# A macaron transformer block: outer FFN tiles and layer tiles driven by one tick counter, new orders, squared chunks summed by TensorE

## The reference

```python
x = x + 0.5 * ffn(layernorm(x), w_up, w_down)
x = x + layers(layernorm(x), ...)
x = x + 0.5 * ffn(layernorm(x), w_up, w_down)

def ternary_linear(x, w):            # the outer FFN's linear
    alpha = mean(abs(w))
    w_q = sign(w) * (abs(w) > 0.5 * alpha)
    rms = sqrt(sum(x * x, -1)) / sqrt(d)
    return (x / (rms + 1e-8)) @ w_q.T
# ffn: h = gelu(ternary_linear(x, w_up)); ternary_linear(h, w_down); 128 -> 512 -> 128

# each of the 8 layers:
Q, K = elu(x @ Wq + bq) + 1, elu(x @ Wk + bk) + 1
value = x @ Wv + bv
KV, Ksum = sum(K * value, 1), sum(K, 1)
V = Q * KV / (Q * Ksum + 1e-6)
x = ln(gelu(V @ Wo + bo) + x)
x = ln(gelu(gelu(x @ W1 + b1) @ W2 + b2) + x)
```

## Time and profile before

| | us |
|---|---|
| median of 3 runs | 959.16 (956.42 to 959.33) |
| the profiled execution's own time | 957.2 |
| its span, first to last instruction | 955.4 |
| busy: PE, DVE, ACT, POOL | 868.9, 870.9, 832.9, 515.1 |
| first outer FFN, until the first layer product | 0 to 101.3 |
| layers, until the last z | 101.3 to 867.0 |
| second outer FFN | 867.0 to 955.4 |

### The profile page before, as it was taken

One profiled execution on the slowest core, in us unless ns is written; L12 is line 12 of the kernel. 1 busy time (PEld: TensorE's weight loads), 2 busy tenths in 40 slices (PEclk: granted clock), 3 DMA queues, 4 the chain that ended last, 5 costly groups with the idle time before them and its releaser, 6 DMA issues.

```text
span 955.4 us, 14548 instructions
## 1 busy us (share of the span) xinstructions
PE 868.9 (91%) x3915; PEld 595.7 (62%) x3915; DVE 870.9 (91%) x3421; ACT 832.9 (87%) x1214; POOL 515.1 (54%) x617
## 2 busy tenths in 40 slices
PE   3986579999999999999999999999999999995887
PEld 2876336666666666666666666666666666553787
DVE  6999669999999999999999999999999999967883
ACT  2754679999999999999999999999999999983653
POOL 4887413555555545555555555455445544554774
PEclk9999679999999999999999999999999999996998
DMA  5000000000000000000000000000000000000011
GB/s 156 1 2 1 25 9 1 1 15 21 1 1 15 21 1 1 15 21 0 1 14 21 1 15 1 20 0 15 1 12 1 1 1 1 0 1 1 12 34 46
DMA packets 19520, 12.07 MB, mean 13 GB/s; under 512 B 1160, under 2 KB 18288, under 8 KB 19440
## 3 DMA queue, kind: packets, MB, share of 16 engines
q1 hardware_dynamic: 19440, 11.13, 4.1%
HBM read 9.03 MB, written 2.10 MB: 12 GB/s over the span
## 4 chain that ended last, share of the span: by engine, by line
ACT 73%; DVE 8%; POOL 7%; PE 6%; issue 5%; DMA 0%; POOLq 0%; SPq 0%; DVEq 0%; ACTq 0%
ACT h L656 16%; ACT x_fm L671 9%; ACT L656 8%; ACT rec L633 6%; ACT rec L642 4%; ACT L679 4%; ACT L697 4%; ACT e_k L623 4%; ACT e_k L616 4%; ACT bank L649 4%; ACT bank L663 3%; ACT e_q L623 3%; ACT e_q L616 2%; DVE z L779 2%; PE bank L368 2%
## 5 line engine op out<-in xcount | busy, mean ns | idle before, releaser
L1167 POOL TENSOR_TENSOR x_lo<-x_fm,x_hi 128x512 fp32r<-128x512 f32 x128 | 172.4, 1347 | 257.3 <-DVE x_hi L932 257.3
L456 PE MATMUL bank<-h,w 128*128 128x512 f32 x512 | 261.1, 593 | 0.5 <-ACT h L656 0.5
L779 DVE TENSOR_SCALAR z<-bank,mv,rstd 128x128 f32<-128x128 f32 x512 | 171.9, 402 | 17.3 <-POOL rstd L1159 17.1
L656 ACT ACTIVATE h<-bank,par 128x512 f32<-128x512 f32 x256 | 170.6, 696 | 1.5 <-PE bank L376 0.6
L374 PE MATMUL bank<-x_hi,w_hi 128*128 128x512 f32 x256 | 159.7, 624 | 13.2 <-ACT h L656 10.2
L1159 POOL TENSOR_TENSOR rstd<-ve,minus_half 128x4 f32<-128x4 f32 x128 | 139.7, 1092 | 10.7
L456 PEld LDWEIGHTS bank<-h,w 128*128 128x128 f32 x512 | 91.7, 190 | 31.5 <-issue 16.5
L765 DVE BATCH_NORM_STATS2 st<-bank 128x6 f32<-128x128 f32 x512 | 111.2, 278 | 0.0
L374 PE MATMUL bank<-x_hi,wqkv_hi 128*128 128x512 f32 x192 | 97.0, 505 | 9.6 <-DVE phi_k L850 7.2
L671 ACT ACTIVATE x_fm<-bank,par 128x512 f32<-128x512 f32 x128 | 97.8, 789 | 7.3 <-PE bank L368 7.3
L376 PE MATMUL bank<-x_hi,w_lo 128*128 128x512 f32 x256 | 101.4, 396 | 0.0
(11 more groups left out here) (105 smaller groups left out, 1924.7 us busy)
## 6 DMA issues: line engine op xcount, KB each, us to landing
x_tm<-in_x SPq DMA_DIRECT2D x8, 256.0 KB, 3.9
raw_w<-in_W SPq DMA_DIRECT2D x8, 256.0 KB, 2.7
w<-in_W SPq DMA_DIRECT2D x8, 256.0 KB, 2.9
out<-x_tm SPq DMA_DIRECT2D x8, 256.0 KB, 2.3
raw_qkv<-in_Wk SPq DMA_DIRECT2D x8, 64.0 KB, 2.5
raw_qkv<-in_Wq SPq DMA_DIRECT2D x8, 64.0 KB, 2.3
raw_qkv<-in_Wv SPq DMA_DIRECT2D x8, 64.0 KB, 2.2
wo<-in_Wo SPq DMA_DIRECT2D x8, 64.0 KB, 2.5
```

The costliest lines, as they stand in the source:

```text
L456: mm = pe.matmul(m.ps_o[:, :], m.w2[T.weights][:, c, :], m.h[:, T.par, c, :], start=c == 0, stop=c == FC - 1)
L656: act.activation(m.h[:, T.par, c, :], m.ps_h[c % 2][:, :], ACT.Gelu_apprx_tanh, bias=column(m, B1, T.layer, c, FC)).then_inc(s.gelu_h[T.pa ...
L779: last = dve.tensor_scalar(dst[:, j, :], src(j), mv[:, j, 0:1], scale[:, j:j + 1], ALU.subtract, ALU.mult)
L1167: pool.tensor_tensor(m.x_lo[:, T.slot, :], m.x_fm[:, T.slot, :], m.x_hi[:, T.slot, :].bitcast(F32), ALU.subtract).then_inc(done, 1)
```

## The change

All three phases now run in one loop over ticks, from FIRST_TICK = -31 to END_TICK = 74, in one function per engine. `l(k, lag)` gives a layer tile, `a(k, lag)` a tile of the first outer FFN and `b(k, lag)` one of the second, two tiles to a tick in each; the lists are new in all of them. The squared chunks are no longer added by GpSimd: `squares` on TensorE accumulates over 16 products of 128x1. The normalisation ahead of the up-products is a scale and a shift on ScalarE (`normal`), with a new `shift` on VectorE. The gelus of the outer FFN have their own buffer fh; hsq is single; the down-products use ps_o alone, in two halves. Who must have emptied a bank is kept in `left` by the build. The exp table is loaded only if another was used. The rounding and x_lo behind the last layer are left out. In the layers the mean of V is one sum and one product.

```diff
+TICKS_IN = NT // 2
+TICK_W1 = 0
+FIRST_TICK, END_TICK = -31, 74
...
+def tiles_of(tick, f):
+    def l(k, lag):
         job = 2 * (tick - lag) + k
         return Tile(job) if 0 <= job < JOBS else None
+    def a(k, lag):
+        t = 2 * (tick - lag + TICKS_IN) + k
+        return Outer(f[0], t) if 0 <= t < NT else None
+    def b(k, lag):
+        t = 2 * (tick - lag - TICKS) + k
+        return Outer(f[1], t) if 0 <= t < NT else None
...
-            if T.n == 1:
-                pe.wait_ge(s.par_ready, 1)
-                pe.wait_ge(f[0].x_new, NT)
-                pe.wait_ge(f[0].ms, NT)
-        pe.wait_ge(s.x_split, T.n)
+        if T.layer == 0:
+            pe.wait_ge(f[0].x_split, T.n)
+        else:
+            pe.wait_ge(s.x_split, T.n - NT)
...
+    def outer_down(F, half):
+        if half == 0:
+            emptied(pe, left, "o")
+            left["o"] = (F.f.x_new, F.n)
+        pe.wait_ge(F.f.gelu[F.par], F.chunks + FC)
+        for j in (2 * half, 2 * half + 1):
+            for c in range(FC):
+                last = pe.matmul(m.ps_o[:, j * P:(j + 1) * P], m.fh[:, F.par, c, j * P:(j + 1) * P],
+                                 m.downT[:, c, :], start=c == 0, stop=c == FC - 1)
...
+    def squares(F):
+        emptied(pe, left, "q")
+        left["q"] = (F.f.ms, F.n)
+        pe.wait_ge(F.f.hsq, F.n)
         for j in range(BLK):
-            last = pe.matmul(m.ps_v[:, j:j + 1], m.hss[:, t % 2, j * P:(j + 1) * P], m.ones[:, 0:1],
-                             start=True, stop=True)
+            for c in range(FC):
+                last = pe.matmul(m.ps_q[:, j:j + 1], m.hsq[:, c, j * P:(j + 1) * P], m.ones[:, 0:1],
+                                 start=c == 0, stop=c == FC - 1)
...
+def load_exp_and_ln(act, tables):
+    if tables["now"] != EXP_AND_LN:
+        act.preload_act_table_set(EXP_AND_LN)
+    tables["now"] = EXP_AND_LN
...
+    def normal(F):
+        at_least(act, F.f.turned_z, F.n - 2)
+        act.wait_ge(F.f.shift, F.n)
+        sc = m.scale[:, F.par]
+        for j in range(BLK):
+            last = act.activation(m.fz[:, F.par, j, :], m.x_tm[:, F.t, j, :], ACT.Identity,
+                                  bias=sc[:, SHIFT, j:j + 1], scale=sc[:, ALPHA, j:j + 1])
+    def square(F):
+        at_least(act, F.f.ssq, F.n - 1)
+        act.wait_ge(F.f.gelu[F.par], F.chunks + FC)
+        act.activation(m.hsq[:, :, :], m.fh[:, F.par, :, :], ACT.Square).then_inc(F.f.hsq, 1)
...
-        for b in range(2):
-            last = dve.tensor_scalar(m.neg_a[:, T.par, b:b + 1], m.kvacc[:, T.par, b:b + 1], m.nrk[:, T.par, b:b + 1],
-                                     column(m, BV, T.layer), ALU.mult, ALU.subtract)
-        last.then_inc(s.neg_a, 1)
+        dve.tensor_tensor(m.neg_a[:, T.par, :], m.kv[:, T.par, :], m.nrk[:, T.par, :], ALU.mult).then_inc(s.neg_a, 1)
     def hi(T, i):
-        if not T:
+        if not T or i == 1 and T.layer == LAYERS - 1:
...
-        pool.tensor_tensor(total, sq[:, 0, :], sq[:, 1, :], ALU.add).then_inc(f.part_sums, 1)
-        pool.wait_ge(f.part_sums, 2 * t + 1)
-        pool.tensor_tensor(total, total, sq[:, 2, :], ALU.add).then_inc(f.part_sums, 1)
-        pool.wait_ge(f.part_sums, 2 * t + 2)
-        pool.tensor_tensor(total, total, sq[:, 3, :], ALU.add).then_inc(f.hss, 1)
```

More of the change, by code:

```diff
@@ L394, in tensor_engine, with emptied, tensor_tick, project @@
     pe.wait_ge(s.ternary_kept, 2)
[L396 to L405, removed]
+    left = {"k": (s.par_kept, 1)}
+    for tick in range(FIRST_TICK, END_TICK):
+        tensor_tick(pe, m, s, f, tick, left)
+def emptied(pe, left, bank):
+    if bank in left:
+        at_least(pe, *left[bank])
+def tensor_tick(pe, m, s, f, tick, left):
+    l, a, b = tiles_of(tick, f)
+    def project(T, i):
         if not T:
@@ new lines, in squares, with turn_c @@
+        last.then_inc(F.f.ssq, 1)
+    def turn_c(F):
+        if not F:
+            return
+        emptied(pe, left, "tz")
+        left["tz"] = (F.f.x_hi, F.n)
+        pe.wait_ge(F.f.z_c, F.n)
+        transpose_tile(pe, m.ps_tz, lambda j: m.fz_c[:, F.par, j, :], m).then_inc(F.f.turned_c, 1)
+    project(l(0, 0), KEY)
+    outer_up(a(0, -26), 1)
+    outer_down(a(0, -25), 1)
+    squares(b(1, 38))
+    up(l(1, 3), 3)
+    turn_c(a(1, -22))
+    turn_y(l(1, 2), 0)
+    down(l(1, 3), 0)
+    turn_y(l(0, 3), 1)
@@ L596, in scalar_engine @@
+    outer_up(a(1, -26), 1)
+    down(l(0, 2), 1)
+    turn_c(a(0, -23))
+    up(l(1, 2), 0)
+    turn(a(0, -27))
+    down(l(0, 2), 2)
+    outer_up(a(1, -26), 2)
+    project_o(l(1, 1))
+    outer_up(a(1, -26), 3)
+    outer_down(b(0, 37), 1)
+    squares(a(0, -26))
+    outer_up(a(0, -27), 0)
+    up(l(1, 2), 1)
+    down(l(0, 2), 3)
+    up(l(1, 2), 2)
+    turn_z(l(1, 3), 1)
+    turn_z(l(0, 1), 0)
+    outer_down(a(0, -26), 0)
 def scalar_engine(act, m, s, f):
@@ new lines, in scalar_tick @@
+    negative(l(0, 0), QUERY)
+    recip(l(1, 1))
+    gelu(b(0, 38), 3)
+    normal(b(0, 37))
+    exp(l(0, 0), QUERY)
+    gelu_h(l(0, 2), 0)
+    gelu_ff(l(1, 3))
+    square(a(0, -25))
+    gelu_h(l(0, 2), 1)
+    gelu(a(1, -25), 0)
+    full(l(1, 2), 0)
+    full(l(0, 3), 1)
+    gelu_o(l(0, 1))
+    gelu_h(l(0, 2), 2)
+    gelu(a(1, -25), 1)
+    square(b(0, 38))
+    gelu(b(1, 38), 0)
+    gelu(a(1, -25), 2)
+    negative(l(1, 0), KEY)
+    gelu_h(l(0, 2), 3)
+    exp(l(1, 0), KEY)
+    negative(l(1, 0), QUERY)
@@ new lines, in scalar_tick @@
+    log_den(l(0, 0))
+    gelu(b(1, 38), 1)
+    exp(l(1, 0), QUERY)
+    z_hi(a(0, -26))
+    gelu(a(1, -25), 3)
+    z_hi(b(0, 37))
+    gelu(b(1, 38), 2)
+    gelu(b(1, 38), 3)
+    gelu_h(l(1, 2), 0)
+    square(b(1, 38))
+    normal(a(1, -26))
+    enter_full(a(0, -22))
+    normal(b(1, 37))
+    gelu_h(l(1, 2), 1)
+    square(a(1, -25))
+    gelu(b(0, 37), 0)
+    gelu_o(l(1, 1))
+    gelu(a(0, -26), 0)
+    gelu_ff(l(0, 2))
+    gelu(b(0, 37), 1)
+    z_hi(a(1, -26))
+    gelu(a(0, -26), 1)
@@ L763, in block_stats @@
+    full(l(1, 3), 1)
+    full(l(0, 1), 0)
+    enter_hi(a(0, -22))
+    gelu_h(l(1, 2), 2)
+    normal(a(0, -27))
+    gelu_h(l(1, 2), 3)
+    enter_full(a(1, -22))
+    gelu(a(0, -26), 2)
+    z_hi(b(1, 37))
+    negative(l(0, -1), KEY)
+    exp(l(0, -1), KEY)
+    gelu(a(0, -26), 3)
+    log_den(l(1, 0))
+    gelu(b(0, 37), 2)
+    enter_hi(a(1, -22))
+    recip(l(0, 0))
 def block_stats(dve, src, st, done):
```

852 lines of the change are left out of this document (403 added, 449 removed).

## The result

The changed kernel takes 1026.76 us (median of 4 runs, 1023.16 to 1031.29) against 957.87 of the kernel before (median of 4, 956.42 to 959.33) beside it: ratio 1.0717, 95% interval 1.0689 to 1.0744. The forecast was 971, its range ended at 988. The profiled execution has a span of 1021.8 us against 955.4, 66.4 more, where I had summed 12.9.

The account below looks back on a forecast made before the run. ScalarE was taken to bound the layers, and a chain of waits through GpSimd's additions and VectorE's normalisations the outer FFNs. Terms 10.5 + 7.4 + 1 - 4 - 2 = +12.9 on 957.2 gave 970.1, forecast 971 us, range 957 to 988.

Parts of the forecast that it names:

- The clock: TensorE in the outer FFNs: dense, it should stay at the high clock, downs 3.73 us instead of 4.61.
- Squares at 0.10 us: TensorE in the outer FFNs: 32 square instructions a tile at 0.10 us, 3.24 us, 2.43 more than before.
- Rival D: Squares on TensorE pack closer, 0.08 us instead of 0.10: 960 us, near no change; chance 0.08.
- First FFN: First outer FFN: last down ends near 100, first layer product at 112 instead of 101.3; +10.5 us (+5 to +15).
- Second FFN: Second outer FFN: 73.8 us from first down to the end against 66.4; +7.4 us (+3 to +12).
- Steady tick: Layers: a tick of two tiles takes 22.96 us against 22.93, 29 ticks; +1 us (-3 to +9).
- Rival B: Layers: the steady tick does not close, its path misses by 0.3 to 0.6 us: 979 to 988; chance 0.20.
- Ramps: Into and out of the layers: out -4 us (-9 to 0), in -2 us (-5 to +3).
- The phases do not overlap: Shared ticks: no tick holds tiles of two phases, so each engine finishes one phase before the next.
- The normalisation on ScalarE: Outer FFNs: four passes, 1.55 us a tile (1.1 to 2.0), hidden behind TensorE; uncovered 25 us.
- The single buffers: Outer FFNs, ps_o and hsq: waits put at nothing; uncovered, the first costs about 1.4 us a tile, 22 in all.
- Rival C: Outer FFNs: the added squares fall into TensorE's idle time and the ramps' -6 decide: 951 us; chance 0.13.

Follow-up runs that it names:

- wide: The changed kernel with each square product multiplying by 128 columns of ones instead of one, same number of instructions: 990.25 us, ratio 1.034 to the kernel before.
- before_wide: The kernel before with 16 square products of 128 columns and no GpSimd additions, its old lists and two down-banks kept: 981.31 us, ratio 1.0235.
- narrow: The changed kernel with 32 columns of ones in each square product instead of one: 1010.32 us, ratio 1.0513 to the kernel before.
- old_layers: The changed kernel with the layers' list entries back in the order and lags of the kernel before: 1022.12 us, ratio 1.0661 to the kernel before.
- attend_first: The changed kernel with attend and a residual ahead of the hi in VectorE's list of the layers: 1026.55 us, ratio 1.07 to the kernel before.
- before_sixteen: The kernel before with 16 square products of one column and no GpSimd additions, its lists and down-banks kept: 1009.55 us, ratio 1.0538.

## Why the prediction was wrong

The direction was right, the size was not: 1026.8 against 971, outside a range that ended at 988. Step by step:

**The clock, the step that failed.** "A dense TensorE should stay at the high one, and the 73.8 assume it." TensorE was dense, busy 84.66 of 84.66 us in the first FFN and 94.27 of 98.87 in the second, and did not stay: 0.84 and 0.76, where wide has 1.00 in both. It cost 33 us: 13.4 in the first FFN (128.91 against 115.51 in wide) and 19.7 in the second (98.87 against 79.18); by the medians wide is 36.5 faster, since the profiled execution was one of the faster of the changed kernel. In the second half of the first FFN even 32 down-products took 5.3 and 6.0 us, where wide takes 3.6. I had used rows of the high clock for everything behind the squares because I saw low-clock rows of before only behind waits, such as the down of 4.61 us, and took the wait for the one cause. No row of before has more than 8 of these instructions together, so the trace could not show it; but that was a reason for a bound from the low rows, which none of my ranges or rivals held. *The Trainium skill, "TensorE: Matmul & The Clock Gate", section "HAM oscillation — how this bites in real kernels", ties the low clock to idle gaps in TensorE's work; by it the dense stretch of the first FFN would have stayed at 2.4 GHz. The trace doesn't agree: 84.66 us busy of 84.66 at a granted clock of 0.84.*

**Squares at 0.10 us.** Measured 0.109 (3.49 for 32, at 55.01). Rival D, 0.08, is dead. *The 81 ns of the Trainium skill, "TensorE: Matmul & The Clock Gate", section "Back-to-back issue gap", do not hold for this form either: wide's instructions with 128 moving columns take 0.109 us.* A pair of tiles takes 19.0 us in wide instead of my 18.5, in the second FFN 20.0 (911.20 to 971.18 for three) instead of 18.7.

**First FFN.** Tile 1's fourth up-chunk ends at 31.2, forecast 30.5. The last down ends at 115.8, forecast 100; in wide 102.4, so the walk was 2.4 short without the clock. The tail from there is 13.1 us, forecast 12: four waits of 1.3 us for x_hi and one of 2.9 for fz_c. In all +27.6 instead of +10.5; wide +14.2, inside my +5 to +15.

**Second FFN.** From the last z's turn to the first down 22.0 us, as forecast (21.9); from there 98.9 instead of 73.8; wide 79.2, which makes +12.7 in all, outside my +12 by 0.7.

**Steady tick.** Rival B came true, beside the clock: 23.27, not 22.96. The path was the one I had walked, with the slow attend at its measured price; I had judged that a miss of 0.15 us at its last link would leave 0.03 a tick. It left 0.34. The price of the term was +1, it measured +9.0: from the recip of tile 4 to that of job 62 it is 674.2 us (183.42 to 857.65), before 665.2. With attend moved, the layers take 760.2 us, and the forecast's 760.8 was for a tick that closes.

**Ramps.** In: the recip of tile 4 stands 54.5 us behind the first product (183.42 less 128.91), as before; forecast 52.5. Out: from the recip of job 62 at 857.65 to the last z's end at 900.81 it is 43.2 us, before 45.9, forecast 41.9 (its rounded terms, 17.6, 15 and 9, add to 41.6). The two ramps together give -2.7 instead of -6.

**What held.** The phases do not overlap (no layer product between up-products). GpSimd's additions are gone and TensorE bounds both FFNs. The normalisation on ScalarE is 0.484 us for each 128x128 pass and 1.64 a tile (forecast 1.55), hidden where TensorE is dense. The single buffers hardly show: down-products wait for nothing in the whole run, where before they waited 12.9 us in all, 6.0 of it in the first FFN; in the second FFN of wide the squares wait 0.3 us for hsq once a pair, 1.2 in all. Rival C was half alive: before_wide shows about half of the added instructions absorbed, but they are too many to be hidden.

Rival C's 951 was reckoned from the profiled execution, without the 1 for the tick and the 1 to the median that my forecast has.

The terms in order of their miss: clock 33, TensorE's rate and the tails of the FFNs 9, tick 8, ramps 3; together the 53 us.

## What to carry to other kernels

In this kernel products with one moving column were not short: they cost as much as those with 128 columns, and in number they took the clock from the work around them, with TensorE busy all the time. Before handing a reduction to TensorE, count such products, try more columns than needed if they must be many (36 us here, for the wider products and the read to match), or add on an engine that has time and leave TensorE the last step. And when an edit moves the time less than its own stage, look at the granted clock of the stages that it doesn't touch.

## What the runs showed of the hardware

The granted clock fell from 2.4 to 1.2 GHz (16 downs of 1.70 us took 3.42) with TensorE 100% busy, behind runs of 32 or 16 fp32 instructions of 128x1, in part behind those of 128x32, and not behind those of 128x128. At the high clock the three forms take the same 0.11 us an instruction. It is not the same from run to run or from one place to the next: of the equal squares at 55.01 and 63.51 only the second was followed by low rows, and two kernels with the same first FFN had 0.93 and 0.79 in the same window. The times follow in some of the kernels: four runs spread over 8.1 us in the changed kernel, 8.4 in narrow and 11.4 in old_layers, but over 1.5 in attend_first and 2.9 in before_sixteen, which have the low clock too; 1.0 in wide and 1.1 in before_wide. What decides which squares are followed by a fall stays open.
